# A graph layer per sample on one core: the class indicator is stored twice, so that two masks and two class terms lie in four row quarters of TensorE; class terms become two column strips; the group's selection work is spread over four steps

## The chip, the cores and the metric

One NeuronCore of a Trainium2 chip runs the whole program. The metric is the device time of one execution in microseconds (us), lower is better. Engines are named as in the profile: PE is TensorE, PEld its weight loads, DVE VectorE, ACT ScalarE, POOL GpSimd, SP SyncE.

## What is computed

`x` is 32 samples of 256 features by 1024 nodes, `adj` a 256 x 256 matrix used as the weight W of both layers, `b1` and `b2` are biases. For each sample:

```
h   = max(layernorm(x, over nodes), 0)
fv  = mean of h over features                # 1024 values
A   = 9 best neighbours by fv_i * fv_j, first dropped, made symmetric, diagonal 1
u   = relu( (A/deg) (W h + b1) )             # over nodes
y   = x + (A/deg) (W u + b2)
```

The similarity is an outer product, so a node's neighbours depend only on the sign class of its own value and on whether it is one of the few extreme nodes. The kernel sorts the nodes of a sample into 8 classes and never forms A: a node of the common class gets a constant plus its own scaled product, the others get a term that depends on their class alone.

## The kernel before

**Tiling.** Partitions hold 128 features, two feature halves per sample; nodes are the free dimension, in two halves `h` of 512, one PSUM bank each. The product W h is made of 12 matmuls per half: `product_hi` (8: `h_hi` with `w_hi` and `w_lo`) and `product_lo` (4: `h_lo` with `w_hi`); ACT makes `h_hi` (`split_h`), POOL the remainder `h_lo` (`split_h` on POOL). Layer 2 does the same with `r_hi` and `r_lo` (`layer2`).

**Classes.** Four samples are a group. Sample `b` of a group owns the 32 partitions `rows_of(b)` of `fv`, `code_r` and `onehot`. Rows 0 to 7 and 8 to 15 of such a quarter both hold the indicator of the classes 0 to 7 (the second set carries the low part of a split value), rows 16 to 31 are unused. For each feature half `m` PE adds a mask matmul onto layer 1's bank (`put_mask`: large negative values on nodes of the other classes, which the relu removes) and a class-term matmul onto layer 2's bank (`put_terms`: `tab` times `onehot`). Both masks of sample b use the row quarter of b, both terms of sample b-1 the one of b-1; `masks_and_terms` issues mask, term, mask, term and waits for `tab_ready` before the first.

**The table.** Each sample's `tab` comes from a chain over four engines: ACT's `relu` leaves sums, POOL's `products` makes `prod`, DVE's `class_terms` reduces it into `src3`, PE's `class_terms` multiplies by `w` into `V2` (one 32-column strip, 256 wide), DVE's `table` makes `v_hi` and `tab`. PE's `class_terms` is the `between` of `layer1(t + 1, 0)`: it stands in the middle of the 8 high products.

**Order.** Each engine's order is written out by hand, in a loop over t (0 to 31). On PE a step t is: `layer1(t+1, 0)` with the class terms of t inside; masks and terms; `layer2(t, 1)`; `layer1(t+1, 1)`; masks and terms; `layer2(t+1, 0)`. DVE's step is `table(t)`, `finish(t, 0)` (the output of half 0), `moments` of a later sample, `finish(t, 1)`, `class_terms(t+1)`, `scales` (which lets ACT normalise). POOL's step is `split_r(t+1, 0)`, `split_h(t+2, 0)`, `products(t+1)`, `split_r(t+1, 1)`, `split_h(t+2, 1)`.

**Group work.** The classes of group k are found during the four steps before it is used; call them by (t+1) mod 4. Before: `column_sums` on PE and `take_sums` on ACT at the end of step 0; `top_first`, `top_next` in step 1; `top_rows`, `gather` (an indirect DMA from POOL's queue, ahead of `products`), `top_mark` in step 2; `codes` and `group_onehot` right behind `table` in step 3, then `transposes`, `group_degrees`, `group_gathered`, `group_sources`; `class_values` and `group_biases` in the next step 0, where POOL makes `tables`. Group 0 is made ahead of the loop, group 1 partly in t = 0.

**Buffers.** `res` has NR = 4 buffers; SP loads one again behind the store that frees it. `pair1` and `pair2` turn over three pairs of PSUM banks, so `layer1(b, 0)` waits for `finish(b-2, 1)` and `layer1(b, 1)` for `finish(b-1, 0)`.

Of the kernel before, what the change touches and what calls it, by code (L numbers as in the profile page):

```python
# [7 lines left out]
F32 = mybir.dt.float32  # L8
# [7 lines left out]
P = 128  # L16
KF = 2
# [5 lines left out]
NR = 4  # L23
# [63 lines left out]
def build(nc, x, x_t, w_t, b1, b2, small, staged, out):  # L87
# [5 lines left out]
    with ExitStack() as ctx:  # L93
# [20 lines left out]
        onehot = sb("onehot", [P, 2, N], F32R)  # L114
# [28 lines left out]
        pre = sb("pre", [P, KF, G, NCLS])  # L143
# [3 lines left out]
        src3 = sb("src3", [P, KF, 32])  # L147
        v_hi = sb("v_hi", [P, S], F32R)
        tab = sb("tab", [P, S], F32R)
# [3 lines left out]
        V2 = aux[:, 0:S]  # L153
# [14 lines left out]
        def rows_of(b):  # L168
            return slice(32 * (b % G), 32 * (b % G) + 32)
# [21 lines left out]
        code_ready = sem("code_ready")  # L191
        onehot_ready = sem("onehot_ready")
# [38 lines left out]
        def sums_of(t):  # L231
            if t == 0:
                return 1
            k = (t + 1) // G + 1
            return k if t > 0 and (t + 1) % G == 0 and k < GROUPS else None

        def group_at(t, step):
            k = (t + 1) // G + 1
            return k if t >= 0 and (t + 1) % G == step and k < GROUPS else None
# [63 lines left out]
        def _(act):  # L303
# [91 lines left out]
            for t in range(LAST):  # L395
# [5 lines left out]
                if t + 2 < NB:  # L401
                    split_h(t + 2, 0)
                relu(t + 1, 1)
                split_r(t + 1, 1)
                if sums_of(t) is not None:
                    take_sums(sums_of(t))
# [10 lines left out]
        def _(pool):  # L417
# [63 lines left out]
            for t in range(-1, LAST):  # L481
# [3 lines left out]
                if group_at(t, 2) is not None:  # L485
                    gather(group_at(t, 2))
# [4 lines left out]
                if t >= 0 and t + 2 < NB:  # L491
                    split_h(t + 2, 1)

        @block.tensor
        def _(pe):
# [44 lines left out]
            def product_hi(bank, mov, n, between=None):  # L540
                for m in range(KF):
                    if m == 1 and between is not None:
                        between()
# [12 lines left out]
            def layer1(b, h, between=None):  # L556
# [7 lines left out]
                product_hi(bank, h_hi, n, between)  # L564
# [3 lines left out]
            def put_mask(b, h, m):  # L568
                q = rows_of(b)
                nc.tensor.matmul(pair1(b, h)[m][:], mask[q, :], onehot[q, (b // G) % 2, half_of(h)], start=False,  # L570
                                 stop=True, tile_position=(q.start, 0), skip_group_check=True).then_inc(l1_done, 1)

            def put_terms(b, h, m):
                q = rows_of(b)
                nc.tensor.matmul(pair2(b, h)[m][:], tab[q, m * P:m * P + P], onehot[q, (b // G) % 2, half_of(h)],  # L575
                                 start=False, stop=True, tile_position=(q.start, 0),
                                 skip_group_check=True).then_inc(l2_done, 1)
# [23 lines left out]
            def class_terms(b):  # L601
# [3 lines left out]
                q = rows_of(b)  # L605
# [5 lines left out]
            def add_terms(b, h):  # L611
                pe.wait_ge(tab_ready, b + 1)
                for m in range(KF):
                    put_terms(b, h, m)
# [16 lines left out]
            for t in range(LAST):  # L631
# [5 lines left out]
                if t > 0:  # L637
                    layer1(t + 1, 0, terms)
                    masks_and_terms(t + 1, 0)
                else:  # L640
                    terms()
                    add_terms(0, 0)
                layer2(t, 1)
                if group_at(t, 3) is not None:
# [3 lines left out]
                masks_and_terms(t + 1, 1)  # L648
                if sums_of(t) is not None:
                    column_sums(sums_of(t))  # L650
# [7 lines left out]
        def _(dve):  # L658
# [120 lines left out]
            def group_biases(k):  # L779
# [3 lines left out]
                if k == 0:  # L783
                    dve.wait_ge(bias_loaded, 32)
                nc.vector.tensor_tensor(
                    pre[:].rearrange("p m g c -> p m (g c)"), X1.rearrange("p m g c -> p m (g c)"),
                    bias1[:].unsqueeze(2).broadcast_to([P, KF, G * NCLS]), ALU.add).then_inc(dve_pre, 1)
                dve.wait_ge(dve_pre, k + 1)
                nc.vector.tensor_scalar(src2[:, :, e, 0:NCLS], pre[:], 0.0, None, ALU.max)
                nc.vector.tensor_tensor(  # L790
                    beta[:, gp], pre[:, :, :, C_COMMON:NCLS:2],
# [3 lines left out]
            def class_terms(b):  # L795
                dve.wait_ge(prod_ready, b + 1)
                for dup in range(2):
                    last = nc.vector.tensor_reduce(src3[:, :, 8 * dup:8 * dup + 8], prod[:], AX_X, ALU.add)  # L798
                last.then_inc(src3_ready, 1)

            def table(b):
                dve.wait_ge(v2_done, b + 1)
                q = rows_of(b)
# [99 lines left out]
```

## Time and profile before

| | us |
|---|---|
| median of 3 runs (lowest, highest) | 597.87 (594.48, 600.29) |
| the profiled execution | 595.5 |
| its span, first to last instruction | 593.7 |
| PE busy in the span | 515.5 (87%) |
| DVE, ACT, POOL busy | 378.5, 341.0, 345.8 |
| mean granted TensorE clock | 0.972 of full |

The profile lists busy time by engine, by source line and tile, what each instruction waited for, and a timeline. A matmul's own duration contains its way through the array: in a stream the next one starts before it ends, so the cost of one is read from start to start. "[1.83 <-DVE src L798]" at the end of a row means that the engine sat idle for 1.83 us before it, and that DVE's instruction of line 798 ended the wait.

### The profile page before, as it was taken

The page shows a single profiled execution, that of the slowest core. Times are in us where ns is not written, and L with a number is a line of the kernel's source. Part 1 is how long each engine was busy: PE and PEld are TensorE (multiplying, and loading weights), DVE is VectorE, ACT ScalarE, POOL GpSimd, SP SyncE. Part 2 cuts the span into 40 slices and gives each one's busy share as a digit, 9 for nine tenths or more (in the row PEclk, how much of TensorE's full clock was granted, in tenths as well). Part 3 has the DMA queues.
Part 4 walks back from the last instruction along what each step waited for, and adds up shares of the span by engine and source line. Part 5 has one row for each costly group of instructions (what it writes and reads, how often), then busy time and mean ns, then how long its engine had stood idle before and what let it go on. Part 6 is the DMA issues. An engine that isn't in the chain of part 4 may idle for free.

```text
span 593.7 us, 6959 instructions
## 1 busy us (share of the span) xinstructions
PE 515.5 (87%) x2288; PEld 341.7 (58%) x2288; DVE 378.5 (64%) x867; ACT 341.0 (57%) x691; POOL 345.8 (58%) x214
## 2 busy tenths in 40 slices
PE   1945968899889988999888989899888998899996
PEld 0334545666556555656556566565556665566664
DVE  5866485847687396865878486874878344752223
ACT  4835764566566566665664756567565643444541
POOL 0444516666555865666566764756676655647772
PEclk9975979999989999999999999999999999999999
DMA  8990544354555534445554445455342323443113
GB/s 331 337 369 2 212 141 159 137 211 165 189 223 212 194 136 180 181 182 201 214 221 145 179 172 189 175 214 213 141 143 85 138 87 127 150 143 141 72 71 141
DMA packets 27683, 102.72 MB, mean 173 GB/s; under 512 B 2048, under 2 KB 2560, under 8 KB 27648
## 3 DMA queue, kind: packets, MB, share of 16 engines
q1 hardware_dynamic: 27264, 101.23, 45.4%
q0 software_dynamic: 384, 1.05, 0.6%
q8 instruction: 18, 0.29, 0.2%
q14 instruction: 17, 0.14, 0.1%
HBM read 68.72 MB, written 33.55 MB: 172 GB/s over the span
## 4 chain that ended last, share of the span: by engine, by line
PE 54%; DVE 23%; POOL 8%; issue 7%; ACT 6%; DMA 2%; DVEq 0%; POOLq 0%; ACTq 0%
PE ps L546 23%; PE ps L552 12%; PE aux L607 5%; DVE res L816 5%; PE ps L570 5%; PE aux L513 4%; POOL h_lo L421 4%; DVE code_r L716 3%; PE aux L501 2%; DVE code L693 2%; ACT r L346 2%; ACT r_hi L361 2%; PE aux L535 2%; DVE fv L691 2%; POOL r_lo L427 1%
## 5 line engine op out<-in xcount | busy, mean ns | idle before, releaser
L427 POOL TENSOR_TENSOR r_lo<-r,r_hi 128x1024 fp32r<-128x1024 f32 x64 | 152.9, 2389 | 171.7 <-ACT r_hi L361 171.1
L816 DVE SCALAR_TENSOR_TENSOR res<-ps,bias,res 128x512 f32<-128x512 f32 x128 | 90.1, 746 | 111.2 <-PE ps L575 111.0
L421 POOL TENSOR_TENSOR h_lo<-hb,h_hi 128x1024 fp32r<-128x1024 f32 x64 | 154.7, 2419 | 10.2 <-ACT h_hi L332 10.2
L546 PE MATMUL ps<-r_hi,w_hi 128*128 128x512 f32 x256 | 109.8, 429 | 2.4 <-ACT r_hi L361 2.4
L546 PE MATMUL ps<-h_hi,w_hi 128*128 128x512 f32 x256 | 105.6, 412 | 6.2 <-DVE res L816 6.2
L314 ACT ACTIVATE hb<-xin,nmean,rstd 128x1024 f32<-128x1024 f32 x64 | 79.0, 1235 | 53.4 <-DVE nmean L677 53.4
L546 PE MATMUL ps<-r_hi,w_lo 128*128 128x512 f32 x256 | 103.0, 402 | 0.0
L546 PE MATMUL ps<-h_hi,w_lo 128*128 128x512 f32 x256 | 101.7, 397 | 0.0
L352 ACT ACTIVATE r<-ps,beta 128x512 f32<-128x512 f32 x64 | 43.4, 684 | 85.4 <-PE ps L570 85.4
L346 ACT ACTIVATE r<-ps,beta 128x504 f32<-128x504 f32 x64 | 43.4, 679 | 82.5 <-PE ps L570 82.5
L664 DVE BATCH_NORM_STATS2 stats<-xin 128x6 f32<-128x512 f32 x128 | 78.8, 679 | 4.7 <-DMA xin<-x 4.7
L546 PEld LDWEIGHTS ps<-r_hi,w_hi 128*128 128x128 f32 x256 | 49.0, 192 | 38.8 <-issue 26.7
L552 PE MATMUL ps<-r_lo,w_hi 128*128 128x512 f32 x256 | 70.4, 397 | 0.0
L552 PE MATMUL ps<-h_lo,w_hi 128*128 128x512 f32 x256 | 70.2, 396 | 0.0
L361 ACT ACTIVATE r_hi<-r 128x1024 fp32r<-128x1024 f32 x64 | 67.9, 1061 | 2.0
L332 ACT ACTIVATE h_hi<-hb 128x1024 fp32r<-128x1024 f32 x64 | 66.8, 1045 | 1.2 <-PE ps L552 1.2
L546 PEld LDWEIGHTS ps<-h_hi,w_hi 128*128 128x128 f32 x256 | 48.3, 189 | 30.3 <-issue 13.6
L607 PE MATMUL aux<-w,src 128*32 128x256 f32 x128 | 34.4, 392 | 28.9 <-DVE src L798 28.9
L552 PEld LDWEIGHTS ps<-r_lo,w_hi 128*128 128x128 f32 x256 | 48.6, 190 | 11.8
L552 PEld LDWEIGHTS ps<-h_lo,w_hi 128*128 128x128 f32 x256 | 48.2, 188 | 11.7
L546 PEld LDWEIGHTS ps<-r_hi,w_lo 128*128 128x128 f32 x256 | 49.3, 193 | 9.0
L546 PEld LDWEIGHTS ps<-h_hi,w_lo 128*128 128x128 f32 x256 | 48.4, 189 | 10.0
(85 smaller groups left out, 590.1 us busy)
## 6 DMA issues: line engine op xcount, KB each, us to landing
xin<-x SPq DMA_DIRECT2D x32, 1024.0 KB, 7.0
res<-x SPq DMA_DIRECT2D x32, 1024.0 KB, 4.9
out<-res SPq DMA_DIRECT2D x31, 1024.0 KB, 4.0
out<-res SPq DMA_DIRECT2D x4, 256.0 KB, 2.1
w<-w_t SPq DMA_DIRECT2D x1, 256.0 KB, 7.9
cst<-small SPq DMA_DIRECT2D x1, 229.5 KB, 5.0
xg<-x_t,rows POOLq DMA_INDIRECT x8, 2.8
r<-staged SPq DMA_DIRECT2D x1, 64.0 KB, 7.4
```

Of the source, the lines that this page charges most:

```text
L314: last = nc.scalar.activation(hb[:, a, kf], xin[:, b % NX, kf], ACT.Relu, bias=nmean[:, kf, e:e + 1], scale=rstd[:, kf, e:e + 1], accum_ou ...
L332: nc.scalar.activation(h_hi[:, :, n], hb[:, b % NH, :, n], ACT.Copy).then_inc(hhi_ready, 1)
L346: nc.scalar.activation(r[:, m, K_TOP:H], bank[m][:, K_TOP:H], ACT.Relu, accum_out=src2[:, m, e, C_COMMON:C_COMMON + 1], **com)
L352: last = nc.scalar.activation(r[:, m, H:N], bank[m][:], ACT.Relu, accum_out=src2[:, m, e, NCLS:NSRC], **com)
L361: nc.scalar.activation(r_hi[:, :, n], r[:, :, n], ACT.Copy).then_inc(rhi_ready, 1)
L421: nc.gpsimd.tensor_tensor(h_lo[:, :, n], hb[:, b % NH, :, n], h_hi[:, :, n].bitcast(F32), ALU.subtract).then_inc(hlo_ready, 1)
L427: nc.gpsimd.tensor_tensor(r_lo[:, :, n], r[:, :, n], r_hi[:, :, n].bitcast(F32), ALU.subtract).then_inc(rlo_ready, 1)
L546: nc.tensor.matmul(bank[m][:], wt[:, kf, m * P:m * P + P], mov[:, kf, n], start=(kf == 0 and wt is w_hi), stop=False, skip_group_check=True)
L552: last = nc.tensor.matmul(bank[m][:], w_hi[:, kf, m * P:m * P + P], mov[:, kf, n], start=False, stop=False, skip_group_check=True)
L607: last = nc.tensor.matmul(V2[q], src3[:, kf], w[:, kf], start=(kf == 0), stop=(kf == KF - 1), tile_position=(0, q.start), skip_group_check ...
L664: last = nc.vector.bn_stats(stats[:, kf, h], xin[:, a, kf, half_of(h)])
L816: nc.vector.scalar_tensor_tensor(res[:, b % NR, m, n], bank[m][:], bias2[:, m:m + 1], res[:, b % NR, m, n], ALU.add, ALU.add).then_inc(out ...
```

## The change

The indicator gets a second copy in the other half of the partitions: `onehot` is now `[P, 2, 2, N]` (group parity, pair of samples, nodes). `group_onehot(k, i)` makes it for 64 partitions with its count, `group_twin(k, i)` writes the same 64 rows, shifted by 64 partitions, without a count. `rows_of(b, m)` is 16 rows at 32 * (b % 2) + 64 * m, so that the masks of t+1 and the terms of t lie in four different row quarters. Masks are issued before the wait for `tab`.

```diff
+        def rows_of(b, m):
+            a = 32 * (b % 2) + 64 * m
+            return slice(a, a + 2 * NCLS)
+
+        def onehot_of(b, q, n):
+            return onehot[q, (b // G) % 2, (b % G) // 2, n]
...
             def masks(b, h):
                 pe.wait_ge(onehot_ready, b // G + 1)
                 for m in range(KF):
-                    put_mask(b, h, m)
-            def masks_and_terms(b, h):
-                pe.wait_ge(onehot_ready, b // G + 1)
-                pe.wait_ge(tab_ready, b)
+                    q = rows_of(b, m)
+                    nc.tensor.matmul(pair1(b, h)[m][:], mask[q, :], onehot_of(b, q, half_of(h)), start=False, stop=True,
+                                     tile_position=(q.start, 0), skip_group_check=True).then_inc(l1_done, 1)
+
+            def add_terms(b, h):
+                pe.wait_ge(tab_ready, b + 1)
                 for m in range(KF):
-                    put_mask(b, h, m)
-                    put_terms(b - 1, h, m)
+                    q = rows_of(b, m)
+                    nc.tensor.matmul(pair2(b, h)[m][:], tab[q, :], onehot_of(b, q, half_of(h)), start=False, stop=True,
+                                     tile_position=(q.start, 0), skip_group_check=True).then_inc(l2_done, 1)
```

PE's class terms stand behind all 8 high products (between `product_hi` and `product_lo`) and are four matmuls of 16 columns by 128, in two column strips, in place of two of 32 by 256. `tab` and `v_hi` become 128 x 128:

```diff
-                product_hi(bank, h_hi, n, between)
+                product_hi(bank, h_hi, n)
+                if between is not None:
+                    between()
...
                 for kf in range(KF):
-                    last = nc.tensor.matmul(V2[q], src3[:, kf], w[:, kf], start=(kf == 0), stop=(kf == KF - 1),
-                                            tile_position=(0, q.start), skip_group_check=True)
+                    for m in range(KF):
+                        q = rows_of(b, m)
+                        last = nc.tensor.matmul(
+                            V2[q], src3[:, kf], w[:, kf, m * P:m * P + P],
+                            start=(kf == 0), stop=(kf == KF - 1), tile_position=(0, q.start), skip_group_check=True)
```

On DVE:

```diff
-            def group_onehot(k):
+            def group_onehot(k, i):
+                q = slice(64 * i, 64 * i + 64)
                 dve.wait_ge(code_ready, 2 * k + 2)
-                nc.vector.tensor_scalar(onehot[:, k % 2], code_r[:], c_("cls"), None, ALU.is_equal, ALU.add,
-                                        accum_out=cnt[:]).then_inc(onehot_ready, 1)
-                dve.wait_ge(onehot_ready, k + 1)
-                nc.vector.tensor_scalar(cnt_d[:], c_("pick_n"), cnt[:], None, ALU.mult).then_inc(cntd_ready, 1)
+                nc.vector.tensor_scalar(onehot[q, k % 2, i], code_r[q], c_("cls")[q], None, ALU.is_equal, ALU.add,
+                                        accum_out=cnt[q]).then_inc(counted, 1)
+                if i == 1:
+                    dve.wait_ge(counted, 2 * k + 2)
+                    nc.vector.tensor_scalar(cnt_d[:], c_("pick_n"), cnt[:], None, ALU.mult).then_inc(cntd_ready, 1)
+
+            def group_twin(k, i):
+                q = slice(64 * i, 64 * i + 64)
+                o = slice(64 - 64 * i, 128 - 64 * i)
+                last = nc.vector.tensor_scalar(onehot[o, k % 2, i], code_r[q], c_("cls")[q], None, ALU.is_equal)
+                if i == 1:
+                    last.then_inc(onehot_ready, 1)
...
-                for dup in range(2):
-                    last = nc.vector.tensor_reduce(src3[:, :, 8 * dup:8 * dup + 8], prod[:], AX_X, ALU.add)
-                last.then_inc(src3_ready, 1)
+                nc.vector.tensor_reduce(
+                    src3[:].rearrange("p k (d c) -> p k d c", d=2),
+                    prod[:].unsqueeze(2).broadcast_to([P, KF, 2, NCLS, NSRC]), AX_X, ALU.add).then_inc(src3_ready, 1)
...
                 table(t)
-                if group_at(t, 3) is not None:
-                    codes(group_at(t, 3))
-                    group_onehot(group_at(t, 3))
                 finish(t, 0)
                 ahead = t + LEAD + 1 if t > 0 else LEAD
                 if ahead < NB:
                     moments(ahead)
-                if t > 0 and group_at(t, 1) is not None:
-                    top_first(group_at(t, 1))
-                finish(t, 1)
-                if t > 0 and group_at(t, 1) is not None:
-                    top_next(group_at(t, 1))
+                if group_at(t, 0) is not None:
+                    top_first(group_at(t, 0))
+                if group_at(t, 1) is not None:
+                    top_rows(group_at(t, 1))
+                if t == 1:
+                    top_rows(1)
+                    top_mark(1)
+                    codes(1)
                 if group_at(t, 2) is not None:
-                    top_rows(group_at(t, 2))
-                    top_mark(group_at(t, 2))
+                    group_onehot(group_at(t, 2), 0)
                 if group_at(t, 3) is not None:
                     group_degrees(group_at(t, 3))
+                finish(t, 1)
+                if group_at(t, 0) is not None:
+                    top_next(group_at(t, 0))
+                if group_at(t, 1) is not None:
+                    top_mark(group_at(t, 1))
+                if group_at(t, 2) is not None:
+                    group_onehot(group_at(t, 2), 1)
+                if group_at(t, 3) is not None:
                     group_gathered(group_at(t, 3))
-                    group_sources(group_at(t, 3))
                 if t + 1 < NB:
                     class_terms(t + 1)
+                if group_at(t, 1) is not None:
+                    codes(group_at(t, 1))
+                if group_at(t, 2) is not None:
+                    group_twin(group_at(t, 2), 0)
+                    group_twin(group_at(t, 2), 1)
+                if group_at(t, 3) is not None:
+                    group_sources(group_at(t, 3))
                 if ahead < NB:
                     scales(ahead)
```

Elsewhere: `column_sums` and `take_sums` of groups 2 to 7 move from the end of step 0 to its middle (on PE between `layer2(t, 1)` and `layer1(t+1, 1)`); POOL's `gather` moves from step 2, ahead of `products`, to the end of step 1; `pre` is no tile of its own any more, `group_biases` works in PSUM; `src3` loses its unused 16 columns; NR falls from 4 to 3. Group 1's onehot halves are made in t = 1 and its degrees in t = 2, as for the others.

## Rows read from the trace of the kernel before

**Rows 1.** Page, busy time by engine: us, share of the span, instructions.
```profile
PE 515.5 (87%) x2288; PEld 341.7 (58%) x2288; DVE 378.5 (64%) x867; ACT 341.0 (57%) x691; POOL 345.8 (58%) x214
```
**Rows 2.** Page, the chain that ended last, share of the span by engine.
```profile
PE 54%; DVE 23%; POOL 8%; issue 7%; ACT 6%; DMA 2%; DVEq 0%; POOLq 0%; ACTq 0%
```
**Rows 3.** Windows, one group of four samples: length, busy by engine, clock, DMA.
```profile
257.70:326.00 68.30, 62.04 (x288) 41.59 (x288) 48.27 (x108) 42.36 (x86) 43.01 (x26) 1.00 0.50 190
```
**Rows 4.** Waits of PE: who waited for whom, us in total, times, longest.
```profile
PE aux L607 <- DVE src L798: 28.9, 14, 2.6
PE aux L535 <- DVE src L774: 9.6, 8, 3.7
PE ps L546 <- DVE res L816: 6.2, 6, 1.0
```
**Rows 5.** Timeline of PE around one masks-and-terms block: start us, us, instruction.
```profile
307.80 0.49 PE L570 MATMUL ps<-onehot,mask 32*128 32x512 f32 x1
307.80 0.50 PE L575 MATMUL ps<-onehot,tab 32*128 32x512 f32 x1
308.13 0.39 PE L570 MATMUL ps<-onehot,mask 32*128 32x512 f32 x1
...
308.46 0.50 PE L546 MATMUL ps<-r_hi,w_hi 128*128 128x512 f32 x1
308.80 0.40 PE L546 MATMUL ps<-r_hi,w_lo 128*128 128x512 f32 x1
```
**Rows 6.** Timeline of PE, class terms and the product behind them.
```profile
304.75 1.05 PE L607 MATMUL aux<-w,src 128*32 128x256 f32 x4 [1.83 <-DVE src L798]
305.73 0.50 PE L546 MATMUL ps<-h_hi,w_hi 128*128 128x512 f32 x1
```
**Rows 7.** Timeline of PE, column sums: first in one strip after another, then four strips in turn.
```profile
12.19 14.58 PE L501 MATMUL aux<-hb,cst 128*32 128x512 f32 x32 [12.19 <-ACT hb L314]
...
332.80 3.64 PE L513 MATMUL aux<-hb,cst 128*32 128x512 f32 x32
```
**Rows 8.** Timeline of DVE and POOL where both are busy.
```profile
349.15 1.04 DVE L685 TENSOR_SCALAR code<-fv 128x1024 bf16<-128x1024 f32 x1
349.60 2.85 POOL L421 TENSOR_TENSOR h_lo<-hb,h_hi 128x1024 fp32r<-128x1024 f32 x1
353.01 2.38 POOL L427 TENSOR_TENSOR r_lo<-r,r_hi 128x1024 fp32r<-128x1024 f32 x1
353.09 2.33 DVE L693 TENSOR_SCALAR code<-code 128x8 bf16<-128x8 bf16 x1
...
374.64 2.39 POOL L421 TENSOR_TENSOR h_lo<-hb,h_hi 128x1024 fp32r<-128x1024 f32 x1
375.04 3.08 DVE L716 SCALAR_TENSOR_TENSOR code_r<-fv,code 128x1023 bf16<-128x1023 f32 x1
378.04 0.15 DVE L718 SCALAR_TENSOR_TENSOR code_r<-fv,code 128x1 bf16<-128x1 f32 x1
```
**Rows 9.** Groups of instructions: the indicator with its count, busy us, mean ns.
```profile
L723 DVE TENSOR_SCALAR_CACHE_REDUCE onehot<-code_r,cst 128x1024 fp32r<-128x1024 bf16 x8 | 10.2, 1279 | 0.3
```
**Rows 10.** Timeline of DVE in a step with top_next, from finish to table.
```profile
350.37 1.41 DVE L816 SCALAR_TENSOR_TENSOR res<-ps,bias,res 128x512 f32<-128x512 f32 x2 [0.17 <-PE ps L575]
...
356.46 0.49 DVE L798 TENSOR_REDUCE src<-prod 128x16 f32<-128x144 f32 x2
...
358.10 0.42 DVE L804 CAST v_hi<-aux 32x256 fp32r<-32x256 f32 x1 [0.70 <-PE aux L607]
358.55 0.47 DVE L806 SCALAR_TENSOR_TENSOR tab<-v_hi,cst,aux 32x256 fp32r<-32x256 f32 x1
```
**Rows 11.** Timeline of POOL in the same step: the products.
```profile
352.43 0.47 POOL L477 TENSOR_TENSOR prod<-src,mix 128x144 f32<-128x144 f32 x1
```
**Rows 12.** Timeline of PE behind its longest wait inside the loop.
```profile
84.40 0.76 PE L570 MATMUL ps<-onehot,mask 32*128 32x512 f32 x1 [4.99 <-DVE tab L806]
...
86.14 0.63 PE L546 MATMUL ps<-r_hi,w_lo 128*128 128x512 f32 x1
```

More of the change, by code:

```diff
@@ L22 @@
 NX = 4
-NR = 4
+NR = 3
 NH = 8
@@ L113, in build @@
         code_r = sb("code_r", [P, N], BF16)
-        onehot = sb("onehot", [P, 2, N], F32R)
+        onehot = sb("onehot", [P, 2, 2, N], F32R)
         w = sb("w", [P, KF, S])
@@ L146, in build @@
         prod = sb("prod", [P, KF, NCLS, NSRC])
-        src3 = sb("src3", [P, KF, 32])
-        v_hi = sb("v_hi", [P, S], F32R)
-        tab = sb("tab", [P, S], F32R)
+        src3 = sb("src3", [P, KF, 2 * NCLS])
+        v_hi = sb("v_hi", [P, P], F32R)
+        tab = sb("tab", [P, P], F32R)
         ps = [pb(f"ps{u}", [P, H]) for u in range(6)]
         aux = pb("aux", [P, 2 * H])
-        V2 = aux[:, 0:S]
+        V2 = aux[:, 0:P]
         XT = aux[:, H:H + S].rearrange("p (k q e) -> p k q e", k=KF, q=G)
@@ L191, in build @@
         code_ready = sem("code_ready")
+        counted = sem("counted")
         onehot_ready = sem("onehot_ready")
@@ L227, in build @@
         block = ctx.enter_context(nc.Block())
[L231 to L235, printed above, removed]
         def group_at(t, step):
             k = (t + 1) // G + 1
-            return k if t >= 0 and (t + 1) % G == step and k < GROUPS else None
+            return k if (t + 1) % G == step and 1 < k < GROUPS or step > 1 and t in (1, 2) and t + 1 == step else None
         def nth(b, h):
@@ L402, in _ @@
                     split_h(t + 2, 0)
+                if group_at(t, 0) is not None:
+                    take_sums(group_at(t, 0))
                 relu(t + 1, 1)
                 split_r(t + 1, 1)
-                if sums_of(t) is not None:
-                    take_sums(sums_of(t))
+                if t == 0:
+                    take_sums(1)
                 if t + 2 < NB:
@@ L492, in _ @@
                     split_h(t + 2, 1)
+                if group_at(t, 1) is not None:
+                    gather(group_at(t, 1))
+                if t == 1:
+                    gather(1)
         @block.tensor
@@ L538, in class_values, with product_hi @@
                 last.then_inc(x1_done, 1)
-            def product_hi(bank, mov, n, between=None):
+            def product_hi(bank, mov, n):
                 for m in range(KF):
-                    if m == 1 and between is not None:
-                        between()
                     for kf in range(KF):
@@ L563, in layer1 @@
                     pe.wait_ge(out_ready, 2 * nth(b - 1, 0))
-                product_hi(bank, h_hi, n, between)
+                product_hi(bank, h_hi, n)
+                if between is not None:
+                    between()
                 pe.wait_ge(hlo_ready, nth(b, h))
                 product_lo(bank, h_lo, n).then_inc(h_used, 1)
[L568 to L577, printed above, removed]
             def masks(b, h):
@@ L638, in _ @@
                     layer1(t + 1, 0, terms)
-                    masks_and_terms(t + 1, 0)
+                    masks(t + 1, 0)
                 else:
                     terms()
-                    add_terms(0, 0)
+                add_terms(t, 0)
                 layer2(t, 1)
+                if group_at(t, 0) is not None:
+                    column_sums(group_at(t, 0))
                 if group_at(t, 3) is not None:
@@ L647, in _ @@
                 layer1(t + 1, 1)
-                masks_and_terms(t + 1, 1)
-                if sums_of(t) is not None:
-                    column_sums(sums_of(t))
+                masks(t + 1, 1)
+                add_terms(t, 1)
+                if t == 0:
+                    column_sums(1)
                 layer2(t + 1, 0)
@@ L819, in _ @@
             nc.vector.memset(unit[:, 0:1], 1.0).then_inc(unit_ready, 1)
-            nc.vector.memset(src3[:], 0.0)
             nc.vector.memset(first[:], PAST)
@@ L836, in _ @@
             codes(0)
-            group_onehot(0)
+            group_onehot(0, 0)
+            group_onehot(0, 1)
+            group_twin(0, 0)
+            group_twin(0, 1)
             group_degrees(0)
```

25 lines of the change are left out of this document (9 added, 16 removed).

## The prediction

> **What bounds the kernel.** I read the busy times first: PE 87%, the others near 60% [rows 1]; then the chain that ended last, which lies on PE for 54% and on DVE for 23% [rows 2]. So PE sets the pace and DVE makes it wait. The windows show a steady beat: four samples, one group, take 68.3 us, at full clock [rows 3], and there are six such groups between 121 and 531 us. PE's waits name three places: class terms wait for DVE's reduce (28.9 us, 14 times, twice a group), class values for DVE's sources (9.6, of which 3.7 once at the start, so 0.85 a group), the high products of half 1 for the output step (6.2, 1.0 a group) [rows 4]. That is 5.9 us a group, 6.5 with the refilling of PE behind each wait; the remaining 61.8 are matmuls. The change works on both parts.
>
> **Matmuls: four in one wave.** A block of masks and terms is two waves: mask and term of m = 0 start together at 307.80, those of m = 1 at 308.13, the next product at 308.46 [rows 5]. A wave costs 0.33; its two matmuls run beside each other because they lie in different row quarters. With four quarters in use one wave should do: -0.33 a block. Blocks: 61 in the loop, add_terms at t = 0 and two at the end: 64, 8 a group. Four row quarters at once are in no row. The bounds: all four beside each other (0.33 in all), or no better than before (0.66). The nearest row is for column strips: 32 column-sum matmuls took 14.6 us one strip after the other and 3.64 with four strips in turn [rows 7], a full factor of four. I take 0.33: -2.6 a group. The Trainium skill ("TensorE: Matmul & The Clock Gate", Part 3) gives 3.07 times for four row tiles, not four, and by it a wave would cost about a third more, 64 x 0.11 = 7 us in all; no row here shows that, and the sum does without it.
>
> **Class terms.** From 304.75 to 305.73 they cost 0.98: four passes 256 wide of about 0.22 and 0.1 for the change of tile shape [rows 6]. After: eight passes 128 wide, in two strips. Side by side (as the strips of [rows 7]) 4 x 0.11 + 0.1 = 0.55; one after another 0.98. I take 0.55: -0.43 a sample, -1.7 a group. Their place behind 8 products in place of 4 costs nothing and brings them 4 x 0.23 = 0.93 later, so DVE has that much longer. The price: only the 4 low products (0.93) and a switch (0.1) stand between V2 and the wave that needs tab. The table chain now takes cast 0.42 plus 0.47 [rows 10]; a finish of 512 columns takes 0.75 (1.41 for two), one table step of 256 takes 0.42 to 0.47, so 128 columns are worth about 0.14: 0.62 and about 0.1 of semaphores. It fits, by 0.3 us, if DVE is free.
>
> A group's matmuls thus fall from 61.8 to 57.5. What PE waits for after the change decides the rest.
>
> **DVE's queue.** I count from E, the end of the second block of a step. PE then does layer 2 (2.8) and 8 products (1.9): it wants src3 at E + 4.8 and tab at E + 6.45. DVE starts finish at E, 1.41 [rows 10]. prod is there at about E + 2.4 (352.9 against E = 350.4 [rows 10, 11]); the reduce takes 0.45 (one of 288 elements for two of 144), table 0.7.
> - *Step 0*: top_next stands before the reduce as it did. It ended at E + 6.1 with the reduce beginning at 356.46 [rows 10]; src3 at E + 6.55, PE waits 1.75 (2.6 before, less the 0.93). The column sums are moved, not added.
> - *Step 1*: top_mark (1.3) runs under the wait for prod; with a later POOL queue (normalise came late) prod is at 3.35, src3 at 3.8, in time. Then codes, which used to stand behind table and now stands between reduce and table. Here the profile shows a mechanism: DVE's L693, 8 elements wide, took 2.33 us and ended with POOL's r_lo (353.01 + 2.38); L716 ended 1.09 behind POOL's h_lo (374.64 + 2.39); and h_lo took 2.85, not 2.4, behind L685 [rows 8]. These operations exclude POOL's. In the new place POOL is always busy: r_lo, then h_lo at once. L716 waits for r_lo (to 5.75) and ends at 6.85. The one-element L718 follows; scales 0.5, table 0.7: tab at 8.2, PE loses 1.75 plus 0.33, as the terms now need a wave of their own: 2.1. If instead POOL's h_lo gets in before L718, add 2.4 less overlap: 4.4.
> - *Step 2*: the counted half indicators cost 1.28 each, taken from the whole one of the same 1024 columns [rows 9]: one hidden before finish, one under the wait for prod. src3 at 4.2, in time. Then the two twins. An uncounted indicator is in no row; nearest is L685 (0.59 from 349.60, when POOL's next was already due, to its end at 350.19) and above 1.28 [rows 8, 9]. As L685 and L693 do, I let it exclude POOL: the first waits for r_lo to 6.15, ends 6.7; h_lo, queued since 6.15, runs to 9.1; the second ends 9.65; scales, table: tab at 10.85. PE loses 4.4 + 0.33 = 4.7. If DVE keeps its turn for the second twin: tab 8.5, loss 2.4. If twins don't touch the port: 0.2 to 1.5.
> - *Step 3*: codes no longer stand before finish(t, 0), so the 1.0 goes; gathered work (1.4) before the reduce fits under prod; sources are ready at 3.7, so the 0.85 goes too. POOL's gather, now last in step 1, no longer holds prod.
> - SP: stores and loads keep their order. With NR = 3 a buffer of res still has two steps, some 26 us, between its store and its next use. ACT: scales come late in steps 0 to 2 and so normalise and relu(t+2, 0), about 1.4 behind the mask; r_hi has 2.9 spare. No cost, but it is why prod comes late.
>
> **The forecast.** One of the two hand-overs goes to POOL (the twins', where the second starts in another quarter than the first) and L718, which starts 0.08 before L716 ends [rows 8], slips in. Waits a group: 1.75 + 2.1 + 4.7 + 0 = 8.6. Group: 57.5 + 8.6 = 66.1, -2.2, six times -13. Start (t = 0 to 3): seven waves and four class terms -4.0; in t = 1 the wait of 4.99 for tab stays, and top_rows, mark, codes and onehot of group 1, some 6 us in t = 1, push finish(1, 1) past its bank's next use: 4.4 in place of 3.8 waits before: +0.6. End: nine waves, four class terms -4.7. The sum on the profiled execution: 595.5 - 13 - 3.4 - 4.7 = 574.4. The median of the runs is 2.4 above the profiled one: 575 to 577, I say 575. Chance 0.35; its own range 567 to 583.
>
> **Rivals.**
> 1. *POOL wins both hand-overs.* Waits 1.75 + 4.4 + 4.7 = 10.9, group 68.4: 588 on the profiled one, 589. For: POOL's operation has been queued for a microsecond when DVE's first ends. Against: [rows 8] show DVE, waiting, taking the port at 349.65 ahead of POOL's next. Chance 0.22. By the Trainium skill ("SBUF — State Buffer", Who interferes with whom) tensor_scalar and two-input operations take an exclusive lock and issue order decides who blocks, which would be this case; the trace agrees as far as the exclusion goes.
> 2. *DVE keeps its turn both times, or the twins leave the port alone.* Waits 1.75 + 2.1 + 2.4 = 6.3, group 63.8: 561; without the port 4.0, group 61.5: 548. Chances 0.20 and 0.10.
> 3. *Slower: the clock.* Behind a wait of 4.99 PE's products took 0.63 in place of 0.40, that is 1.2 in place of 2.4 GHz, about 2.3 us in all [rows 5, 12]; behind 1.83 to 2.6 they did not. Rival 1 has two waits of 4.1 to 4.4 a group. If each ends so, 12 x 2.3 = 28 more: 616. It decides from some 12.2 us of waits a group, about one drop in three of rival 1's waits. Chance 0.07.
> 4. *The strips and quarters don't run side by side*: 64 x 0.33 = 21 back on the forecast: 596. Against it [rows 5, 7]. Chance 0.06.
>
> **Numbers.** 1% of 597.9 puts the bounds at 591.9 and 603.9; less than that a measurement can't tell from none. Faster: 0.35 + 0.18 of rival 1 + 0.30 = 0.82. Same: rival 4 and the upper edge of rival 1: 0.10. Slower: 0.08. The range holds the forecast, rival 1, the first half of rival 2: 550 to 592.
>
> **What would show it.** In the profile after: one wave (four matmuls starting within some 0.02 us) in blocks of half 1, 0.33 to the next product; class terms 0.55; PE busy down by some 30 us. No PE wait in step 3; the rest of the waits for tab (L806), not for src. In step 2 one twin of 2.5 to 3 us. Wrong would be: twins of about 0.6 or 1.1 with POOL running (rival 2), a L718 of over 2 us (rival 1), granted clock below 0.95 in the group windows (rival 3), four matmuls in two steps (rival 4).

## The result and the profile after

Slower by a little: 600.82 us against 596.75 (medians of 20 runs each on the same chip), ratio 1.0055, 95% interval 1.0033 to 1.0077. Ratios here and below are of mean times, so they differ a little from those of the medians, and leave out one run of x1_waves (631.8 us) that fell in a slower state of the chip. The forecast was 575, range 550 to 592: the time lies above the range, by 9 us. The profiled execution took 600.94 (before: 595.5), 26.5 us above the 574.4 to which the forecast was summed; its span is 599.1 (before: 593.7). The mean granted clock of TensorE is 0.926 in place of 0.972.

I read the same views as before the change. The page, busy time by engine and the chain that ended last:
```profile
PE 514.8 (86%) x2416; PEld 351.5 (59%) x2416; DVE 418.1 (70%) x866; ACT 339.2 (57%) x691; POOL 353.2 (59%) x214
...
PE 60%; DVE 29%; ACT 4%; POOL 3%; DMA 2%; issue 2%; DVEq 0%; POOLq 0%; ACTq 0%
```
PE was busy for 515.5 us [rows 1] and still is, although the change took matmul time away. DVE has 40 us more to do and holds 29% of the chain in place of 23% [rows 2].

The windows, each about one group. Columns: window, its length, busy us (instructions) of PE, PE's weight loads, DVE, ACT and POOL, the granted clock, DMA share, GB/s. After:
```profile
191.00:261.00 70.00, 62.54 (x305) 43.40 (x305) 54.57 (x109) 42.35 (x87) 44.04 (x26) 0.95 0.49 185
...
330.80:401.90 71.10, 63.67 (x303) 44.16 (x302) 54.24 (x108) 42.02 (x86) 43.98 (x27) 0.93 0.48 179
```
A group took 68.3 at a clock of 1.00 [rows 3]. It now takes 70.5, by the starts of the first and the last column sums of six (five groups in 352.4 us):
```profile
122.61 3.64 PE L517 MATMUL aux<-hb,cst 128*32 128x512 f32 x32
...
475.01 3.64 PE L517 MATMUL aux<-hb,cst 128*32 128x512 f32 x32
```
In none of six windows of 70 us between 121 and 541 is the clock 1.00: 0.93 to 0.95. In the same six stretches of the kernel before it is 0.98 once and 1.00 five times. That is the line that decides this case.

PE's waits, who for whom, us in total, times, longest:
```profile
PE ps L585 <- DVE tab L810: 34.8, 14, 4.5
PE aux L603 <- DVE src L802: 16.6, 13, 1.9
...
PE ps L548 <- DVE res L820: 0.8, 1, 0.8
```
Against [rows 4]: the wait for the sources in step 3 is gone from the loop, so is the one for the output step, as forecast. The class terms' wait for the reduce has fallen from 28.9 to 16.6, and 34.8 now stand at the table, where 6.0 stood before.

**Where a group's time went.** I followed PE from the start of each product to the start of the next, in the group 330.80 to 401.90. Of its 71.1 us, 58.0 are matmuls at full clock (forecast 57.5), 8.6 are waits (1.88 + 3.23 + 0.77 + 2.69; forecast 8.6) and 4.5 are matmuls that ran at 1.2 in place of 2.4 GHz (forecast 0). The timeline of PE in that group shows both stretches of the last kind: start us, us, instruction, [wait <- releaser].
```profile
362.82 0.50 PE L578 MATMUL ps<-onehot,mask 16*128 16x512 f32 x2
366.06 0.50 PE L585 MATMUL ps<-onehot,tab 16*128 16x512 f32 x2 [2.74 <-DVE tab L810]
366.49 0.50 PE L548 MATMUL ps<-r_hi,w_hi 128*128 128x512 f32 x1
...
367.14 0.63 PE L548 MATMUL ps<-r_hi,w_hi 128*128 128x512 f32 x1
...
369.70 1.39 PE L554 MATMUL ps<-r_lo,w_hi 128*128 128x512 f32 x4
370.94 0.40 PE L548 MATMUL ps<-h_hi,w_hi 128*128 128x512 f32 x1
...
384.26 0.79 PE L585 MATMUL ps<-onehot,tab 16*128 16x512 f32 x2 [2.20 <-DVE tab L810]
384.99 0.80 PE L548 MATMUL ps<-r_hi,w_hi 128*128 128x512 f32 x1
...
388.57 1.91 PE L554 MATMUL ps<-r_lo,w_hi 128*128 128x512 f32 x4
```
A product of 0.40 becomes one of 0.63. The eight high products take 3.21 and 3.58 from first start to the next line's, in place of 1.96; the four low ones 1.24 and 1.71 in place of 0.94. Before the change a wait of 2.54 had no such sequel: the products behind it took 0.40 each.
```profile
357.01 1.05 PE L607 MATMUL aux<-w,src 128*32 128x256 f32 x4 [2.54 <-DVE src L798]
...
358.33 0.40 PE L546 MATMUL ps<-h_hi,w_lo 128*128 128x512 f32 x1
```
But the kernel before isn't free of it. One wait of 1.83 inside its loop was followed by the lower clock, and another of 1.83, two groups on [rows 6: 304.75 and 305.73], was not:
```profile
167.85 1.81 PE L607 MATMUL aux<-w,src 128*32 128x256 f32 x4 [1.83 <-DVE src L798]
...
170.19 0.63 PE L546 MATMUL ps<-h_hi,w_lo 128*128 128x512 f32 x1
```
After the change it is the same with waits of 1.80, of which there are six in the loop. Two have such a sequel, four don't:
```profile
277.10 0.62 PE L603 MATMUL aux<-w,src 128*16 128x128 f32 x8 [1.80 <-DVE src L802]
...
280.51 0.63 PE L548 MATMUL ps<-r_hi,w_lo 128*128 128x512 f32 x1
```
Summed over the trace after, matmuls that were stretched in this way cost 30.0 us (start to start, above their usual time), 22.2 of them in twelve places between 121 and 541. Before it was 5.6 in three places, 1.6 of it in that stretch.

**Who makes the table late.** DVE and POOL in steps 1 and 2 of that group:
```profile
359.73 3.03 DVE L711 SCALAR_TENSOR_TENSOR code_r<-fv,code 128x1023 bf16<-128x1023 f32 x1
362.68 2.30 DVE L713 SCALAR_TENSOR_TENSOR code_r<-fv,code 128x1 bf16<-128x1 f32 x1
...
377.19 2.28 DVE L724 TENSOR_SCALAR cnt_d<-cst,cnt 128x32 f32<-128x32 f32 x1
379.38 0.44 DVE L802 TENSOR_REDUCE src<-prod 128x32 f32<-128x288 f32 x1
379.86 3.21 DVE L729 TENSOR_SCALAR onehot<-code_r,cst 64x1024 fp32r<-64x1024 bf16 x2
```
```profile
359.28 2.38 POOL L429 TENSOR_TENSOR r_lo<-r,r_hi 128x1024 fp32r<-128x1024 f32 x1
361.64 3.32 POOL L423 TENSOR_TENSOR h_lo<-hb,h_hi 128x1024 fp32r<-128x1024 f32 x1
...
377.03 2.40 POOL L429 TENSOR_TENSOR r_lo<-r,r_hi 128x1024 fp32r<-128x1024 f32 x1 [0.56 <-ACT r_hi L361]
379.38 2.37 POOL L423 TENSOR_TENSOR h_lo<-hb,h_hi 128x1024 fp32r<-128x1024 f32 x1
```
L711 waits for r_lo (to 361.66) and ends 1.10 behind it. Then POOL's h_lo, queued since 361.64, takes the turn, and L713, one element wide, ends with it: 2.30 in place of 0.15 [rows 8]. In step 2 cnt_d, 32 wide, ends with r_lo, and the first twin with h_lo. The second twin follows in 0.75: nothing of POOL's was queued behind h_lo.

### The profile page after: what moved, and what is told of

It reads as the page before. It is cut to its first block, busy times and chain, and to the rows that moved or that the text cites. A ratio compares the mean times of both kernels' runs of the same rounds, so it can differ in the third digit from the quotient of the medians.

```text
span 599.1 us, 7152 instructions
## 1 busy us (share of the span) xinstructions
PE 514.8 (86%) x2416; PEld 351.5 (59%) x2416; DVE 418.1 (70%) x866; ACT 339.2 (57%) x691; POOL 353.2 (59%) x214
## 4 chain that ended last, share of the span: by engine, by line
PE 60%; DVE 29%; ACT 4%; POOL 3%; DMA 2%; issue 2%; DVEq 0%; POOLq 0%; ACTq 0%
PE ps L548 29%; PE ps L554 15%; PE aux L517 4%; DVE res L820 4%; PE ps L578 4%; DVE onehot L729 4%; DVE code_r L711 3%; DVE cnt_d L724 2%; DVE code L688 2%; DVE code_r L713 2%; POOL h_lo L423 2%; PE ps L585 2%; PE aux L603 2%; DVE stats L659 2%; DVE fv L686 2%
## 5 line engine op out<-in xcount | busy, mean ns | idle before, releaser
L423 POOL TENSOR_TENSOR h_lo<-hb,h_hi 128x1024 fp32r<-128x1024 f32 x64 | 158.8, 2483 | 10.0 <-ACT h_hi L332 10.0
L548 PE MATMUL ps<-r_hi,w_hi 128*128 128x512 f32 x256 | 120.0, 469 | 3.3 <-ACT r_hi L361 3.3
L548 PE MATMUL ps<-r_hi,w_lo 128*128 128x512 f32 x256 | 112.2, 438 | 0.0
L548 PE MATMUL ps<-h_hi,w_hi 128*128 128x512 f32 x256 | 102.7, 401 | 0.8 <-DVE res L820 0.8
L554 PE MATMUL ps<-r_lo,w_hi 128*128 128x512 f32 x256 | 75.8, 421 | 0.0
L554 PE MATMUL ps<-h_lo,w_hi 128*128 128x512 f32 x256 | 74.3, 413 | 0.0
L548 PEld LDWEIGHTS ps<-r_hi,w_hi 128*128 128x128 f32 x256 | 54.4, 212 | 32.1 <-issue 16.7
L585 PE MATMUL ps<-onehot,tab 16*128 16x512 f32 x128 | 33.9, 530 | 34.9 <-DVE tab L810 34.8
L548 PEld LDWEIGHTS ps<-r_hi,w_lo 128*128 128x128 f32 x256 | 55.3, 216 | 10.5
L554 PEld LDWEIGHTS ps<-r_lo,w_hi 128*128 128x128 f32 x256 | 53.2, 208 | 13.4
```

What stands on the lines that cost most here:

```text
L423: nc.gpsimd.tensor_tensor(h_lo[:, :, n], hb[:, b % NH, :, n], h_hi[:, :, n].bitcast(F32), ALU.subtract).then_inc(hlo_ready, 1)
L548: nc.tensor.matmul(bank[m][:], wt[:, kf, m * P:m * P + P], mov[:, kf, n], start=(kf == 0 and wt is w_hi), stop=False, skip_group_check=True)
L554: last = nc.tensor.matmul(bank[m][:], w_hi[:, kf, m * P:m * P + P], mov[:, kf, n], start=False, stop=False, skip_group_check=True)
L585: nc.tensor.matmul(pair2(b, h)[m][:], tab[q, :], onehot_of(b, q, half_of(h)), start=False, stop=True, tile_position=(q.start, 0), skip_gro ...
```

## The experiments

The theory once the trace was read: the new waits come from DVE operations that exclude POOL's, and a second part of the loss from TensorE's clock behind them. Rivals: the quarters and strips themselves are the loss; the new places of the group work are. Ratios are to the kernel before, on the same chip, with 95% intervals. The kernel after stands at 1.0055.

**The change's two halves.** `x1_waves`: the kernel before with the doubled indicator, quarters and strips, and the group work at its old places, the twins last in step 3.
```diff
-                         accum_out=cnt[:]).then_inc(onehot_ready, 1)
+                         accum_out=cnt[q]).then_inc(counted, 1)
...
+            def group_twin(k, i):
...
-                put_terms(b - 1, h, m)
```


> The kernel before with the matmul part of the change alone (four row quarters, class terms in two strips behind the 8 high products, the 128-wide table, one reduce); the group work stays where it was, the twins stand behind class_terms in step 3. Theory (the loss comes from where the group work stands, not from the waves): 6.97 + 6.23 us of matmuls a sample as in the changed kernel, waits of about 1.7, 1.0 and 1 to 4 a group, no loss of clock, so about 63 us a group and 560 to 572 us in all. Rival (the twins and the wider table cost DVE as much as the waves give PE): 590 or more, with PE waiting for tab in every step.


Measured 619.34, ratio 1.039 (1.031 to 1.047).

`x2_spread`: the kernel before with the group work at the new places, and one row quarter per sample as before, so no twins.
```diff
+                if group_at(t, 0) is not None:
+                    top_first(group_at(t, 0))
...
+                if group_at(t, 1) is not None:
+                    codes(group_at(t, 1))
```


> The kernel before with the respread group work alone: old quarters, old class terms in the middle of the high products, no twins, one wait for tab ahead of masks and terms; group_biases works in PSUM and NR is 3. Theory: codes and cnt_d still stand between reduce and table and still lose the port to POOL, so PE waits for tab about 2.7 us in one step and for src 1 to 3 in three, and the clock falls behind them: 70 to 73 us a group, 605 to 620 in all. Rival (the respread itself is good and only the twins spoil it): under 590.


Measured 613.39, ratio 1.029 (1.022 to 1.035).

PE's waits of the first, then of the second:
```profile
PE aux L533 <- DVE cnt_d L720: 22.5, 7, 4.7
...
PE ps L584 <- DVE tab L806: 12.5, 9, 4.5
```
```profile
PE aux L609 <- DVE src L805: 25.9, 14, 2.6
PE ps L572 <- DVE tab L813: 21.1, 7, 5.0
```
Each half alone is slower than before, and slower than both together. My expectation of x1_waves fell. With the old places both counted halves of the indicator lie in step 3 ahead of cnt_d, for which PE waits seven times, some 3.0 each (4.7 the last time); the respread is there to take that away. The respread alone came out as expected. It pays for codes between reduce and table (some 2.7 a group at the table; the 5.0 at t = 1 was there before) and has no cheaper matmuls to show for it. So the loss can't be put on one half alone: each needs the other, and together they come near to breaking even.

**Filling the wait.** `x3_fill`: after, with 8 matmuls of a zero tile between masks and class terms in steps 1 and 2 (16 in t = 1). They add zero to the banks of layer 2.
```diff
+                    if t > 1 and group_at(t, 2) is not None or group_at(t, 3) is not None:
+                        fillers(t, 8)
```


> The changed kernel with matmuls of a zero stationary tile (8 of 512 columns, 16 at t = 1) between masks and terms in the steps where PE waits for tab; they add zero to a bank that is open. Theory (the clock, not the waits, is the last third of the loss): the waits stay as long (table comes when it comes), but the products behind them run at 2.4 GHz; 4.3 us a group and some 4 at the start come back: 568 to 578 us, granted clock 0.97 or more. Rival (the low clock stands for something else, or the fillers only move it): 595 to 605, clock 0.93.


`x10_fill2`: the same with 11, 13 and, in t = 1, 20.


> The changed kernel with more matmuls of the zero tile in the waits for tab: 11, 13 and 20 in place of 8, 8 and 16, so that hardly any idle time is left there; DVE's work and tab's time are the same. Theory (the low clock behind the waits is some 4 us a group, of which the shorter filling gave back less than half): clock 0.97 or more, 66 to 67 us a group, 572 to 580. Rival (the shorter filling already gave back all that the clock is worth): 586 to 592.


Measured 588.94, ratio 0.987 (0.981 to 0.993), and 589.78, ratio 0.986 (0.981 to 0.991). Work that computes nothing makes the kernel 1.8% and 2.0% faster than after (0.987 and 0.986 against 1.0055). The mean clock rises from 0.926 to 0.961 and 0.963, and the stretched matmuls cost 10.6 and 7.3 us between 121 and 541, in place of 22.2: 12 and 15 us less, where the runs gained 11 and 12. Both expectations had asked for more, because I had put all of the clock's price behind the waits for the table. In x3_fill the first products behind such a wait do keep their 0.40, though in three of the six groups the last ones lose it (from 309.35 in the rows below); in x10_fill2 none does. But in both the lower clock now follows the class terms' wait of 1.80 four times, where it followed it twice in after:
```profile
303.77 2.13 PE L585 MATMUL ps<-w_hi,zero_w 128*128 128x512 f32 x8
307.38 0.49 PE L592 MATMUL ps<-onehot,tab 16*128 16x512 f32 x2 [1.48 <-DVE tab L821]
...
308.14 0.40 PE L550 MATMUL ps<-r_hi,w_lo 128*128 128x512 f32 x1
...
309.35 0.63 PE L550 MATMUL ps<-r_hi,w_hi 128*128 128x512 f32 x1
```
```profile
270.72 0.62 PE L610 MATMUL aux<-w,src 128*16 128x128 f32 x8 [1.80 <-DVE src L813]
...
274.26 0.63 PE L550 MATMUL ps<-r_hi,w_lo 128*128 128x512 f32 x1
```

**Three small operations.** `x4_noport`: after, with cnt_d and the twins written as the form that also adds up its output, into a tile that nobody reads, and the last element of code_r with the code as a scalar per partition.
```diff
-  tensor_scalar(cnt_d[:], c_("pick_n"), cnt[:], None, ALU.mult)
+  tensor_scalar(cnt_d[:], c_("pick_n"), cnt[:], None, ALU.mult, ALU.add, accum_out=spare[:, 0:1])
-  tensor_scalar(onehot[o, k % 2, i], code_r[q], c_("cls")[q], None, ALU.is_equal)
+  tensor_scalar(onehot[o, k % 2, i], code_r[q], c_("cls")[q], None, ALU.is_equal, ALU.add, accum_out=spare[o, 1:2])
-  scalar_tensor_tensor(code_r[:, N - 1:N], fv[:, 0:1], 0.0, code[:, 0:1], ALU.min, ALU.add)
+  tensor_copy(col0[:], code[:, 0:1])
+  tensor_scalar(code_r[:, N - 1:N], fv[:, 0:1], 0.0, col0[:], ALU.min, ALU.add)
```


> The changed kernel with three DVE instructions in forms that should not exclude POOL: the twins and cnt_d write an accumulator as well, the last code_r element takes its code as a per-partition scalar. DVE does the same work otherwise. Theory (the waits are the port): L713 falls from 2.30 to 0.2, cnt_d from 2.28 to 0.25, the twins cost 1.28 each whatever POOL does; the tab wait falls from 2.8 to 0.7 in one step and from 2.2 to about 1.2 in the next, src's 0.7 goes, and the clock stays up: 550 to 562 us. Rival (DVE simply has too much to do between reduce and table): its sum falls by little and the time stays above 590.


Measured 554.79, ratio 0.933 (0.927 to 0.940), in the middle of what was expected. Groups of instructions (count, busy us, mean ns), one group's window, and PE's waits:
```profile
L735 DVE TENSOR_SCALAR_CACHE_REDUCE onehot<-code_r,cst 64x1024 fp32r<-64x1024 bf16 x16 | 20.4, 1275 | 0.4
...
L729 DVE TENSOR_SCALAR_CACHE_REDUCE cnt_d<-cst,cnt 128x32 f32<-128x32 f32 x8 | 2.0, 248 | 0.3
L718 DVE TENSOR_SCALAR code_r<-fv,col 128x1 bf16<-128x1 f32 x8 | 1.7, 216 | 0.3
```
```profile
245.30:308.00 62.70, 59.11 (x307) 40.94 (x306) 49.72 (x113) 42.06 (x87) 43.88 (x26) 1.00 0.54 204
```
```profile
PE ps L588 <- DVE tab L817: 15.6, 14, 4.5
...
PE aux L606 <- DVE src L809: 11.2, 7, 1.8
```
The group takes 62.7, of which 58.1 are matmuls, as in after, and 4.6 waits; the clock is back at 1.00. So of the 8.4 that this group is shorter than the one above, 3.9 are waits and 4.5 clock. In two of the six groups a wait of 1.80 is still followed by the lower clock, 1.5 us each time.

The three alone. `x7_last`: the last element only.


> The changed kernel with the last code_r element alone in the form that leaves the port to POOL. Theory (each blocked instruction has its own price: its stay plus the clock behind it): L713 2.30 to 0.2, that step's wait for tab from 2.8 to about 0.7 and its 1.5 us at the low clock gone, the next step as it was: 3.6 us a group, 574 to 582. Rival (the two steps are coupled, DVE then meets POOL elsewhere and the wait moves to the next step): 590 or more.


`x8_cntd`: cnt_d only.


> The changed kernel with cnt_d alone in the form that leaves the port to POOL. Theory: the 0.7 us wait for src in step 3's first half goes; but the twins come 2 us earlier, while POOL's r_lo still runs, so they wait in cnt_d's place and tab is little earlier: 590 to 598. Rival (cnt_d's 2.3 us come back whole): 3 to 5 us a group with the clock, 570 to 582.


`x9_twin`: the twins only.


> The changed kernel with the two twins alone in the form that leaves the port to POOL. Theory (cnt_d and the twins share one wait for POOL's r_lo: taking it from one gives it to the other): the twins take 2.6 in place of 3.2 us, tab comes 0.6 earlier, perhaps a little less low clock: 592 to 598. Rival (the twins are the ones that hold POOL up and the gain of all three forms is mostly theirs): 580 or less.


Measured 583.32, ratio 0.979 (0.972 to 0.986); 603.65, ratio 1.013 (1.005 to 1.020); 597.61, ratio 0.998 (0.993 to 1.003). The third is as expected, the first 1.3 us above its range, the second 5.7 above. Against after that is 2.7 points better, 0.7 worse and 0.8 better (the interval of the second holds the ratio of after, so its 0.7 is within the noise), 2.7 in all as they stand (2.67, 0.71 and 0.76), where the three at once bring 7.2. What one of them leaves, the next picks up. In x7_last the wait for the table falls in one group from 2.74 to 0.86 in step 1 and rises in step 2 from 2.20 (with 0.69 for the reduce ahead of it) to 3.51. The twins in x8_cntd and the row that answers to it in after:
```profile
L732 DVE TENSOR_SCALAR onehot<-code_r,cst 64x1024 fp32r<-64x1024 bf16 x16 | 34.3, 2144 | 0.4
```
```profile
L729 DVE TENSOR_SCALAR onehot<-code_r,cst 64x1024 fp32r<-64x1024 bf16 x16 | 24.1, 1504 | 0.4
```
With cnt_d out of the way the twins run into POOL's operation instead and wait the longer.

**Another order on PE.** `x5_reord`: after, with the high products of half 1 of layer 2 between masks and class terms in steps 1 and 2, so that PE has 1.9 us to do before it wants the table.
```diff
+                if group_at(t, 2) is not None or group_at(t, 3) is not None:
+                    layer2(t, 1, lambda: add_terms(t, 0))
```


> The changed kernel with PE's order alone changed in the two steps with the waits for tab: the high products of layer2(t, 1) stand between masks and terms of half 0. DVE's blocked instructions stay. Theory (what hurts is that PE stands idle behind them, and then the clock): the 8 products fill 2 of the 2.8 and 3 us and keep the clock; per group 3.5 us of waits and 4 of clock less: 552 to 566. Rival (the late output step then stops layer1(t + 1, 1), and late scales stop the relu): 585 or more, with new waits on DVE's output or on r_hi.


Measured 575.28, ratio 0.965 (0.958 to 0.972): faster, by less than expected. The waits for the table fall from 34.8 to 16.1, but the high products now wait 6.1 for the output step, where it was 0.8: with the class terms issued later, layer 2's banks come free later (argued from the order, not tried by itself).
```profile
PE ps L585 <- DVE tab L815: 16.1, 12, 2.4
...
PE ps L548 <- DVE res L825: 6.1, 8, 2.7
```
`x6_both`: the forms of x4_noport and this order.


> The kernel without the port conflicts (as in the run before with all three forms, 554.8 us) and with PE's new order. Theory: only 0.8 and 1.1 us of wait a group are left to hide and a separate wave costs 0.2 to 0.3 each time: 549 to 555. Rival: the separate wave and the later terms cost more than they hide, 556 to 562.


Measured 550.21, ratio 0.923 (0.917 to 0.929), as expected.

**Without the respread.** `x11_wavesnoport`: x1_waves with the three forms of x4_noport.


> The matmul part of the change alone (as in the run of 619 us) with the last code_r element, cnt_d and the twins in the forms that leave the port to POOL; group work as before the change. Theory (with the doubled indicator the old place in step 3 is too late: codes, two halves, two twins and the degrees lie in one step and PE waits for cnt_d and for the indicator): 600 to 615. Rival (the respread is not needed once the port is free): 585 or less.


Measured 611.66, ratio 1.023 (1.018 to 1.028), as expected. PE still waits for cnt_d, 20.2 us in 7 times. With the doubled indicator and the old places the three forms alone don't bring the gain.

**The best version.** `x12_topnext`: x6_both with the one operation of this kind that both kernels have, the 8-wide update of the codes in top_next (2.33 in [rows 8]), in the adding form too.
```diff
-  tensor_scalar(code[:, 1:K_TOP + 1], code[:, 1:K_TOP + 1], 2.0, None, ALU.add)
+  tensor_scalar(code[:, 1:K_TOP + 1], code[:, 1:K_TOP + 1], 2.0, None, ALU.add, ALU.add, accum_out=spare[:, 0:1])
```


> The fastest version so far (550.2 us: three forms that leave the port and PE's new order) with the 8-element code update of top_next in the same accumulating form. Theory: it falls from 2.33 to 0.2 us, src3 comes 2 us earlier in step 1's first half and the wait of 1.8 us there goes, six times: 538 to 543. Rival (prod comes late there too, so that the wait changes its name): 547 to 551.


Measured 537.10, ratio 0.897 (0.893 to 0.901), a little better than expected and 10.3% faster than before. A group's window, the operation itself, and two of the waits that are left. Both for the table stand near the start, at 61.5 and 83.3; so does the longest for the output step, at 95.6:
```profile
238.70:298.80 60.10, 59.56 (x307) 40.77 (x308) 47.35 (x114) 42.03 (x87) 43.97 (x26) 1.00 0.56 212
```
```profile
L696 DVE TENSOR_SCALAR_CACHE_REDUCE code<-code 128x8 bf16<-128x8 bf16 x8 | 1.3, 158 | 0.0
```
```profile
PE ps L551 <- DVE res L833: 6.0, 7, 2.7
...
PE ps L588 <- DVE tab L823: 3.2, 2, 2.4
```

## Why the prediction was wrong

**The step that failed** is the price of the waits in the forecast: "Waits a group: 1.75 + 2.1 + 4.7 + 0 = 8.6. Group: 57.5 + 8.6 = 66.1". The sum of the waits came out right, and the clock behind them was set at nothing. The drop was kept for a rival with waits above 4 us ("behind 1.83 to 2.6 they did not"), deciding from 12.2 us a group. It came at 8.6, behind waits of 2.74 and 2.20, at 1.5 and 3.0 a drop in the group shown (2.3 taken), on average 3.7 us a group in the loop. That rival, with a chance of 0.07, is what happened, at shorter waits. Stretched matmuls cost 24.4 of the 26.5 us by which the sum was short (30.0 against the 5.6 already in the trace before); the matmuls at full clock, 0.5 a group, some 3; the waits and the start give about 1 back. The evidence against the drop was also misread: of the waits of 1.83 in the kernel before, the one that ends at 167.85 is followed by it, and so is one of 2.41 near the start (54.91). It was easy to miss there: the group with the drop at 167.85 took 68.64 from column sums to column sums and the next one 68.26, although the stretch itself cost 1.6. That the waits, 8.6, came out as forecast is luck, as steps 1 and 2 below show. The second half of rival 2, the twins leaving the port alone, gave 548. With the twins alone in such a form, x9_twin, it was 597.6; that sum also counts cnt_d as nothing and lets L718 slip in, and x4_noport, in which all three are free, took 554.8.

**Four in one wave**: right in kind, sized too well. The four start together and the next product follows after 0.44:
```profile
340.79 0.49 PE L578 MATMUL ps<-onehot,mask 16*128 16x512 f32 x2
340.80 0.50 PE L585 MATMUL ps<-onehot,tab 16*128 16x512 f32 x2
341.23 0.50 PE L548 MATMUL ps<-r_hi,w_hi 128*128 128x512 f32 x1
```
Two waves had cost 0.66 [rows 5]: -0.22 a block, not -0.33, which is 7 us less than forecast over 64 blocks. Smaller savings that the sum left out make up for part of it (the class values' matmuls take 0.90 in place of 1.01), so that a group's matmuls are only 0.5 above forecast. The nearest row, for column strips [rows 7], was the wrong kin. The Trainium skill ("TensorE: Matmul & The Clock Gate", Part 3) gives 3.07 times for four row tiles, by which two masks and two class terms would take 0.33 x 4 / 3.07 = 0.43, an estimate from that page; the trace agrees with it.

**Class terms**: 0.98 to 0.55 (from 361.14 to 361.69), as forecast. **Step 3**: its waits are gone, as forecast. **Step 0**: 1.88 against 1.75.

**Step 1**: 3.23 against 2.1. I let L718 (now L713) slip in before POOL; POOL won, which was half of rival 1.

**Step 2**: 0.77 + 2.69 = 3.46 against 4.7. The second twin was to lose its turn and didn't. In its stead cnt_d, which I had counted as nothing, waited for r_lo and held the reduce back by the 0.77. The errors of steps 1 and 2 nearly cancel in the sum of the waits.

**The port.** That plain tensor_scalar and two-input operations exclude POOL's is shown by x4_noport: the same results in the adding form take 248 and 1275 ns with POOL running as before. The Trainium skill ("SBUF — State Buffer", Who interferes with whom) states this lock, and leaves out of it the tensor_scalar form that writes its accumulator; the trace agrees. I had cited the lock and had not asked which form escapes it.

**Start and end** were to give 3.4 and 4.7. The five groups between the first and the last column sums cost 10.8 more (352.4 against 341.7), the whole span 5.4 more. So the rest, which holds the sixth group too, gave 5.4 back, in place of 10.3 (8.1 and the 2.2 of a group).

**What stays open**: which of these waits has a drop behind it. In after two waits of 1.80 at the same place of the loop have one and four have none; a wait of 2.53 (at 296.46) and one of 2.09 (at 508) have none, 2.20 has one. So neither the length of a wait nor its place in the order decides it. x3_fill and x10_fill2 made the drops fewer and moved some without ending them, and no kernel here varied the work ahead of a wait by itself. Nor were NR = 3 and the new place of gather tried alone; PE waits for a transfer once in either trace, for the first gather (8.1 us before, 7.5 after, ahead of the loop), so no loss of the groups points at them.

## What to carry to other kernels

On an engine that sets the pace a wait costs its length and whatever the clock loses behind it: price both. Before writing that a wait has no sequel, go through all waits of that length in the trace: here the exception was in it. And take no rule for the clock from one kernel to another order of its work. Before halving matmuls by doubling an operand, ask which engine writes the copy, and whether its form of instruction shuts out a neighbour; a one-element operation can cost as much as the neighbour's longest. When such operations stand in a row, change all of them: one at a time here gave 2.7 points, together 7.2.

## What the hardware showed beyond what was expected

- Two DVE operations back to back can lose the turn: at 362.68 a queued POOL operation got in between them, and a DVE operation of one element took 2.30 us.
- The adding form costs more when nothing is in its way (1275 ns for 1024 columns against 0.75 us for a twin) and far less otherwise (158 ns against 2.33 us for 8 columns).
- Reading X1 straight from PSUM in the relu for src2 cut that operation from 959 to 225 ns on average (L789 before, L794 after), which the forecast had not counted. It is the port again: while POOL's h_lo ran, the form that reads SBUF took 1.06 to 1.09 us and ended with h_lo, the one that reads PSUM 0.22 to 0.23; with POOL idle the SBUF form took 0.20 (x1_waves).
- Matmuls of a zero tile, some 0.26 us each, made the kernel 1.8% faster, with a mean clock of 0.961 in place of 0.926.
